# A two-block transformer kernel: first phase and first expert layer in one program block, and another order at the entry of the second attention

## The reference

```python
h = _layernorm(x) * (1 + ca) + sa
x = x + ga * _L0_attn_ref(h, W_qkv, W_out)           # linear attention, 16 heads of 8
h = _layernorm(x) * (1 + cb) + sb
x = x + gb * _L0_ffn_ref(h, ...)                     # the best of 8 experts per token, 128 -> 512 -> 128
h = _layernorm(x) * (1 + ca) + sa                    # modulation of block 1 from here
x = x + ga * _L1_attn_ref(h, Wqkv, Wproj, lambdas)   # differential attention, causal, 32 query and 8 key heads
# qkv = h @ Wqkv; softmax of q k^T / sqrt(8), pairs of heads subtracted with lambda, times v; two products with Wproj
h = _layernorm(x) * (1 + cb) + sb
x = x + gb * _L1_ffn_ref(h, ...)                     # the best two of 8 experts
```

## Time and profile before

| | us |
|---|---|
| median of 3 runs (643.12 to 646.38) | 644.96 |
| profiled execution | 643.2 |
| its span | 641.4 |
| PE busy | 513.7 |
| DVE busy | 422.1 |
| ACT busy | 335.7 |
| POOL busy | 320.8 |

### The profile page before, as it was taken

One profiled execution on the slowest core, in us unless ns is written; L12 is line 12 of the kernel. 1 busy time (PEld: TensorE's weight loads), 2 busy tenths in 40 slices (PEclk: granted clock), 3 DMA queues, 4 the chain that ended last, 5 costly groups with the idle time before them and its releaser, 6 DMA issues. The chain is left out here.

```text
span 641.4 us, 12683 instructions
## 1 busy us (share of the span) xinstructions
PE 513.7 (80%) x3814; PEld 349.8 (55%) x3814; DVE 422.1 (66%) x1650; ACT 335.7 (52%) x561; POOL 320.8 (50%) x481
## 2 busy tenths in 40 slices
PE   4977559970747999997999999999746199999970
PEld 2656449870323344543454444444445199999970
DVE  3775545446347979997899999993545745455436
ACT  5653325430752367775677777777434054444423
POOL 2541057772263356664468557754420267777630
PEclk9998569995687589998999999999955599999995
DMA  9300011123174445555544454332074011111205
GB/s 336 156 2 34 33 32 53 50 54 103 21 134 79 97 106 108 114 123 124 119 118 104 121 127 106 81 76 59 19 280 124 17 44 52 47 49 52 47 30 196
DMA packets 87899, 58.18 MB, mean 91 GB/s; under 512 B 72469, under 2 KB 73622, under 8 KB 85946
## 3 DMA queue, kind: packets, MB, share of 16 engines
q1 hardware_dynamic: 79258, 40.85, 25.5%
q0 software_dynamic: 3968, 8.13, 4.8%
q10 hardware_dynamic: 4608, 8.39, 3.7%
HBM read 37.72 MB, written 19.63 MB: 89 GB/s over the span
## 5 line engine op out<-in xcount | busy, mean ns | idle before, releaser
L1591 DVE CUSTOM_DVE_ANT_1 banks<-banks,a_mask 128x480 f32<-128x480 f32 (+14 forms) x480 | 190.0, 459 | 18.6 <-PE banks L1806 16.7
L1712 ACT ACTIVATE a_prob_<-banks 128x1024 f32<-128x1024 f32 x160 | 155.7, 1023 | 60.7 <-PE banks L1820 60.7
L1505 POOL TENSOR_SCALAR_AFFINE_SELECT a_prob_<-a_prob_ 128x512 f32<-128x512 f32 x128 | 81.0, 635 | 88.7 <-ACT a_prob_ L1712 88.6
L1806 PE MATMUL banks<-a_k_u_,a_q_u_ 72*128 72x512 bf16 (+15 forms) x512 | 109.2, 309 | 11.8 <-DMA a_k_u_<-scratch_k_parts 5.9
L1806 PEld LDWEIGHTS banks<-a_k_u_,a_q_u_ 72*128 72x128 bf16 x512 | 65.2, 149 | 81.8 <-DVE a_neg_max_ L1591 42.6
L1820 PE MATMUL banks<-a_q_u_,a_k_x_ 75*128 75x512 bf16 x320 | 102.2, 401 | 5.4 <-DMA a_q_u_<-scratch_m_rows 4.5
L1190 PE MATMUL banks<-f_hgt,f_w_now 128*112 128x128 f32 (+1 forms) x808 | 103.0, 279 | 0.4 <-DVE f_w_now L1013 0.3
L1190 PEld LDWEIGHTS banks<-f_hgt,f_w_now 128*112 128x112 f32 (+1 forms) x808 | 96.4, 185 | 1.3 <-DVE f_w_now L1013 0.8
L943 POOL DMA_INDIRECT f_hg<-scratch_h_rows,r_source x62 | 60.1, 970 | 71.6 <-DVE r_source L292 33.9
L1832 PE MATMUL banks<-a_prob_,a_v_g_ 128*32 128x512 f32 (+3 forms) x1024 | 86.0, 454 | 0.0
L949 POOL DMA_INDIRECT scratch_back_rows<-f_y,r_home x62 | 61.0, 984 | 35.3 <-DVE f_y L1039 26.5
(11 more groups left out here) (229 smaller groups left out, 633.6 us busy)
## 6 DMA issues: line engine op xcount, KB each, us to landing
a_q_u_<-scratch_q_parts SPq DMA_DIRECT2D x16, 576.0 KB
scratch_o_rows<-a_o_sb_ ACTq DMA_DIRECT2D x28, 256.0 KB, 2.6
w<-in_w SPq DMA_DIRECT2D x2, 2048.0 KB, 10.1
...
```

The costliest lines, as they stand in the source:

```text
L1505: nc.gpsimd.affine_select(out=block_p, in_=block_p, pattern=[[0, JH], [1, P]], compare_op=ALU.is_ge, fill=0.0, base=0, channel_multiplier= ...
L1591: last = nc.vector.tensor_tensor_reduce(out=found, in0=found, in1=mask[:, :, TG - 4 * (t + 1):], scale=-1.0, scalar=-MASKED, op0=ALU.add, ...
L1712: nc.scalar.activation(prob[g % 2][:, 2 * e:2 * e + 2].rearrange("p s j t c -> p (s j) t c"), PS[:, b0:b0 + 2, :].rearrange("p s (j c t) - ...
L1806: last = nc.tensor.matmul(PS[:, a % 3, off:off + width], queries[:, g % 2, :, t], k_u[r][:, :, g % 2 * TG:g % 2 * TG + 4 * (t + 1)], start ...
```

## The change

1. `phase_first` and the expert layer 0 become one program block: `experts_programs` returns the five engines' programs, and `phase_first` appends them to its own. The barrier between them goes; PE and ACT wait for the experts' numbers by a semaphore (`eid_ready`).
2. At the end of the first phase the lines of batch 2 are computed ahead of the residual of batch 3, `back` and `ranks` change places on PE, and two steps on ACT.
3. The loads of `back_rows`, the scaling and the addition move from the expert layer behind the barrier into the attention, batch by batch (`scaled_rows`, `added`), between the steps of the norm. Batch 0's norm is shared by ACT and DVE.
4. PE gets twenty products of constants (128x128 by 128x256, bfloat16, result unused) as soon as batch 0's rows have arrived, ahead of its first transposes.
5. Batch 0 goes through products and parts before batch 1; its lowest part is made on DVE (`lowest_first`); both of its first units are staged before batch 1's parts are written. The products of batches 2 and 3 each move behind one group of maxima.
6. On POOL the lowest parts of batch 3 and the weights scaled by the gate (`wproj_b`) move behind groups 1 and 2 of the loop.
7. In the loop SP issues `maxima_in(g + 1)` ahead of `stage`.
8. The query features of the first phase (`q_feat`) lie in the memory of `xn`, which is free by then.

The diff, without the re-indented body of the expert layer:

```diff
@@ -432,7 +432,7 @@
         qr = buf("qr", [P, B, T])
-        q_feat = buf("q_feat", [P, B, T])
+        q_feat = xn[:].rearrange("p (b i) d -> p b (i d)", i=NI)
@@ -461,6 +461,8 @@
         nd_of = PS[:, 4:6, :].rearrange("p a (c n) -> p (a c) n", c=2)
+        end_phase(sb)
+        sync, gpsimd, vector, scalar, tensor = experts_programs(nc, dram, sb, ps, 0, router, ctx)
@@ -615,8 +619,8 @@
             residual(2)
+            router.norm.lines(ve, 2)
             residual(3)
-            router.norm.lines(ve, 2)
@@ -701,10 +706,11 @@
             router.normalise(ac, 3)
+            router.rows_back(ac, 2)
             router.modulate(ac, 3)
-            router.rows_back(ac, 2)
...
             router.weights(ac)
+            scalar(ac)
@@ -840,16 +846,17 @@
             router.logits(pe, 2)
+            router.back(pe, 2)
...
             router.logits(pe, 3)
-            router.back(pe, 2)
+            router.ranks(pe, 1)
             router.back(pe, 3)
-            router.ranks(pe, 1)
...
-def phase_experts(nc, dram, sb, ps, layer, router):
+            tensor(pe)
...
+def experts_programs(nc, dram, sb, ps, layer, router, ctx):
@@ -1300,6 +1304,8 @@
         w_in, lam_in, wproj_ready = (semaphore(n) for n in ("w_in", "lam_in", "wproj_ready"))
+        back_in = [semaphore(f"back_in{b}_") for b in range(B)]
+        moved_ready, tail_ready, lo0_ready = (semaphore(n) for n in ("moved_ready", "tail_ready", "lo0_ready"))
@@ -1322,6 +1328,8 @@
         areas = ((P, slice(0, 2)), (D // 2, slice(2, 3)))
+        back = [at[b][:].rearrange("p (i d) -> p i d", i=NI) for b in range(B)]
+        moved = [o_b[b // 2][:, b % 2, :].rearrange("p (i d) -> p i d", i=NI) for b in range(B)]
@@ -1346,15 +1354,22 @@
             sp.dma_start(mask[:], dram["amask"]).then_inc(lam_in, 16)
+            for landed, count in sb["y_out"]:
+                sp.wait_ge(landed, count)
+            for b in range(B):
+                sp.dma_start(back[b], dram["back_rows"][b * T:(b + 1) * T, :].rearrange("(p i) d -> p i d", i=NI)
+                             ).then_inc(back_in[b], 16)
...
-                ready = (hi_ready, mid_ready, lo_ready)[n]
-                sp.wait_ge(ready, 2 * b + 1)
+                ready, of = (hi_ready, mid_ready, lo_ready)[n], b
+                if n == PARTS - 1:
+                    ready, of = (lo_ready, b - 1) if b else (lo0_ready, 0)
+                sp.wait_ge(ready, 2 * of + 1)
...
                                  part[b % 2][:, n, half, :].rearrange("f (u t) -> f u t", t=TG)).then_inc(parts_out[b], 16)
-                sp.wait_ge(ready, 2 * b + 2)
+                sp.wait_ge(ready, 2 * of + 2)
@@ -1428,20 +1443,23 @@
-            for b in range(2):
-                for n in range(PARTS):
-                    write_part(b, n)
-                stage(b)
+            for n in range(PARTS):
+                write_part(0, n)
+            stage(0)
+            stage(1)
             values(0)
+            for n in range(PARTS):
+                write_part(1, n)
...
             for g in range(GROUPS):
+                if g + 1 < GROUPS:
+                    maxima_in(g + 1)
...
                 if g + 1 < GROUPS:
-                    maxima_in(g + 1)
@@ -1525,15 +1543,11 @@
                 norm.deviations(gp, b)
-            gp.wait_ge(w_in, 2 * 16)
-            for b in range(B - 1):
-                lowest(b)
+            lowest(1)
...
             split_maxima(0)
-            lowest(B - 1)
-            for b in range(B):
-                nc.gpsimd.tensor_tensor(wproj_b[:, b, :], wproj[:], gates[:, b, 1, 0, :], ALU.mult).then_inc(wproj_ready, 1)
+            lowest(2)
@@ -1542,6 +1556,12 @@
                     causal(g, kb)
+                if g == 1:
+                    lowest(B - 1)
+                if g == 2:
+                    gp.wait_ge(w_in, 2 * 16)
+                    for b in range(B):
+                        nc.gpsimd.tensor_tensor(wproj_b[:, b, :], wproj[:], gates[:, b, 1, 0, :], ALU.mult).then_inc(wproj_ready, 1)
@@ -1556,12 +1576,44 @@
                 q = b % 2
-                if b >= 2:
-                    ve.wait_ge(lo_ready, 2 * (b - 1))
+                if b == 2:
+                    ve.wait_ge(lo0_ready, 2)
+                if b == 3:
+                    ve.wait_ge(lo_ready, 2)
...
+            def scaled_rows(b):
...
+                ve.wait_ge(back_in[b], 16)
+                for i in range(NI):
+                    t = b * NI + i
+                    ch.step(nc.vector.scalar_tensor_tensor(moved[b][:, i, :], back[b][:, i, :], sb["gate0"][:, 0, t:t + 1],
+                                                           gates[:, b, 0, 1, :], ALU.mult, ALU.mult))
...
+            def added(b):
...
+                ch.wait()
+                xb = x_sb[:, b * NI:(b + 1) * NI, :]
+                nc.vector.tensor_tensor(xb, xb, moved[b], ALU.add).then_inc(moved_ready, 1)
+                ve.wait_ge(moved_ready, b + 1)
+                norm.variances(ch, b)
...
+            def shared_rows():
...
+                for t in (2, 3):
+                    last = nc.vector.tensor_scalar(xn[:, t, :], x_sb[:, t, :], norm.mv[:, t, 0:1], norm.rstd[:, t:t + 1],
+                                                   ALU.subtract, ALU.mult)
+                last.then_inc(tail_ready, 1)
...
+            def lowest_first():
...
+                for n, (rows, at_) in enumerate(areas):
+                    ve.wait_ge(mid_ready, n + 1)
+                    nc.vector.tensor_tensor(part[0][0:rows, 2, at_], rest[0][0:rows, at_], part[0][0:rows, 1, at_],
+                                            ALU.subtract).then_inc(lo0_ready, 1)
@@ -1627,27 +1679,33 @@
-            norm.variances(ch, 0)
-            norm.variances(ch, 1)
+            scaled_rows(0)
+            added(0)
+            scaled_rows(1)
             norm.lines(ve, 0)
-            norm.variances(ch, 2)
+            shared_rows()
+            added(1)
+            scaled_rows(2)
             norm.lines(ve, 1)
-            norm.variances(ch, 3)
+            added(2)
             norm.lines(ve, 2)
-            norm.lines(ve, 3)
             remainders(0)
-            remainders(1)
-            remainders(2)
+            lowest_first()
+            scaled_rows(3)
+            added(3)
...
             nc.vector.memset(one_row[:], 1.0).then_inc(lam_sum, 1)
+            norm.lines(ve, 3)
+            remainders(1)
...
                 maximum(0, a)
+            remainders(2)
+            for a in range(NA):
+                maximum(1, a)
...
             coefficients()
-            for a in range(NA):
-                maximum(1, a)
@@ -1730,22 +1788,26 @@
-            norm.normalise(ac, 0)
+            ac.wait_ge(norm.line_ready, 1)
+            for t in (0, 1):
+                last = nc.scalar.activation(xn[:, t, :], x_sb[:, t, :], ACT.Identity, scale=norm.rstd[:, t:t + 1],
+                                            bias=norm.line[:, t:t + 1])
+            last.then_inc(norm.xn_ready, 1)
+            rows_t(0)
             norm.normalise(ac, 1)
-            rows_t(0)
+            highest(0)
+            middle(0)
...
             norm.normalise(ac, 2)
-            highest(0)
+            highest(1)
+            middle(1)
+            rows_t(2)
             norm.normalise(ac, 3)
-            middle(0)
-            highest(1)
-            rows_t(2)
-            middle(1)
-            highest(2)
             rows_t(3)
-            middle(2)
...
             nc.scalar.activation(lexp[:], lsum[:], ACT.Exp).then_inc(lam_exp, 1)
+            highest(2)
+            middle(2)
@@ -1834,24 +1898,29 @@
+            pe.wait_ge(back_in[0], 16)
+            for n in range(20):
+                nc.tensor.matmul(PS[:, 0, 0:2 * P], sb["ones"], sb["squares"][:].rearrange("p n c -> p (n c)"), start=True, stop=True)
...
             pe.wait_ge(w_in, 2 * 16)
-            for b in range(B - 1):
-                transposed(b + 1)
-                products(b)
+            products(0)
+            transposed(1)
+            products(1)
+            transposed(2)
+            transposed(3)
...
                 max_scores(0, a)
-            products(B - 1)
+            products(2)
+            for a in range(NA):
+                max_scores(1, a)
+            products(3)
...
             nc.tensor.matmul(PS[:, 7, 0:2], one_row[:], lexp[:], start=True, stop=True).then_inc(lam_mm, 1)
-            for a in range(NA):
-                max_scores(1, a)
...
             pe.wait_ge(fills, RING + 2 * VR)
-            pe.wait_ge(wproj_ready, B)
@@ -1887,6 +1956,8 @@
                     pe.wait_ge(upd_ready, b)
+                else:
+                    pe.wait_ge(wproj_ready, B)
...
```

589 lines of the change are left out of this document (295 added, 294 removed).

## The result

The changed kernel takes 628.46 us (median of 4, 627.51 to 629.26) where the kernel before took 645.67 beside it (median of 4, 643.12 to 648.41): a ratio of 0.973, interval 0.969 to 0.978. The forecast was 628.0. Its profiled execution took 628.5 us for a span of 626.7, 14.7 us less than the span of before.

What follows compares the result with a forecast made beforehand. Stages with different limits: POOL in the expert layer, PE in the attention loop. 3.1 + 0.8 + 5.7 - 0.4 + 7.2 = 16.4, plus 0.5: 16.9 us off 644.96 gives 628.1, said as 628, range 624.5 to 632.

Steps and rivals of the forecast that it cites:

- First phase: End of the first phase: batch 2's earlier line and the new PE order gain 3.1 us, bounds 2 and 5.
- first seam: Entry to the expert layer: without a barrier the first gather follows the row numbers directly, gaining 0.8 us.
- Loads behind the weights: Attention entry: semaphore clearing, barrier and SP's four weight loads make the expert rows 1.4 us later, bounds 0.8 and 3.
- T: Moment the expert rows' data is there at the attention's entry, forecast near 150.4 us in the old trace's time.
- First maxima: Attention entry: first row-maximum products at 179.1 us for 189.35, 10.2 us earlier, about 34 us after the last scatter's issue.
- What is given back: Attention entry: batch 3's products behind group 1 are uncovered, shrinking the gain from 10.2 to 5.7 us at first scores.
- The loop's loads: Attention loop: maxima issued ahead of the staging remove PE's stall; 7.2 us gained, bounds 3 and 7.8.
- Warm start of the loop: First groups of the attention loop: starting at full clock would gain about 0.5 us.
- A: Loop's stall stays or moves to the value rows; 7 us missing, 635 us; chance 0.15.
- B: Attention entry gives all back, batch 3's products costing 6 us more than reckoned; 634 us; chance 0.11.
- C: Loop starts at lasting full PE clock, DVE becomes the limit, about 4 us more saved; 624 us; chance 0.10.
- D: Slower than before: early loop groups stay at half clock, each costing 3.2 us; 650 us; chance 0.02.

Runs made afterwards that it cites:

- e5: Changed kernel with the line of batch 2 behind the residual of batch 3 again on DVE; 634.59 us, 0.984 of the kernel before.
- e4: Changed kernel with SP issuing the four loads of expert rows ahead of the four weight loads; 627.32 us, 0.973 of the kernel before.
- e3: Changed kernel without its twenty products of constants, on a slower chip; 655.41 us, 0.975 of the kernel before on that chip.
- e1: Changed kernel with the loop's staging ahead of the next group's maxima again, on a slower chip; 664.32 us, 0.987 of the kernel before there.
- e6: Changed kernel with the products of batches 2 and 3, and their remainders, one place earlier; 628.27 us, 0.974 of the kernel before.
- e2: Kernel before with one edit, the next group's maxima loaded ahead of the staging, on a slower chip; 661.35 us, 0.984 of the unedited kernel there.

## Why the prediction was right, and where its sum was not

The sum was 16.9 us, the traces give 14.7. That the time still came out within 0.5 us of the median is luck. The prediction started from a median 1.8 us above the profiled execution of before and carried this difference over; the changed kernel does not show it (profiled 628.5, median 628.46). With the 14.7 us of the traces the same working gives 630.3. The medians are 17.2 us apart, and where the slower executions of before lost the rest no trace shows. The mechanisms hold for the most part, and single terms missed both ways:

- **First phase, 3.1, and first seam, 0.8.** The total is right, 3.7 for 3.9, and so are the causes: the line (e5) and the barrier, 1.81 - 1.06 = 0.75 from the row numbers to the gather. The sizes within the phase cancelled. Batch 2's transposes came 3.63 us sooner, 0.46 of it since the batch ahead was sooner by that much (56.99 for 57.45). The new order on PE cost 7.33 - 6.40 = 0.93 up to the logits of batch 3, for 0.4, and gave back 0.27 behind them, for 0.4. So the logits at 70.10 (forecast 70.1) are luck in part.
- **Loads behind the weights, 1.4 us later.** T came 5.76 after the last scatter for 4.11, so 1.65 (forecast 5.5, measured 5.8). The weights' four issues, 1.5 us, are the cause: e4 takes it back. Ahead of them, the semaphore clearing and the barrier took 0.93 us together (141.39 to 142.32), where some 0.9 were reckoned.
- **First transposes, T + 5.8.** 5.76.
- **Twenty products, 0.2.** Right that they are hidden (4.45 us under a forecast bound of 5.0). In this trace they gave nothing, transposes and query products ran at half clock; in five others they may have given up to 0.9 us (e3, e4), within the bounds.
- **First maxima, 34.2 us after the last scatter.** 35.98: the term that was mis-sized. The last write before the staging was issued at 167.22 + 0.66 = 167.88, 26.5 us after the last scatter, where 169.9 - 144.91 = 25.0 was forecast. Of these 1.5 us T makes 0.3, query parts at T + 12.1 for 12.7 take 0.6 off, and SP's writes make 0.5. The rest, 1.3, is what was wrong in the working: it summed remainders, middle and lowest parts (4.2 us) as if one engine took over from the other at once, while the trace has 5.6 from the start of the highest part's cast to the end of the lowest, with DVE idle for 0.99 us ahead of the remainders (ACT's cast takes 1.01) and for 0.94 ahead of the lowest part (ACT's middle part). From the write to the maxima it took 9.5 us and not 8.7, and the 0.5 us that were to be lost to batch 3's transposes were not. In e1 and e3 another 1.2 us went with SP's issuing of the writes, so the 1.8 us in all are of the size of the scatter.
- **What is given back.** The step was right: from first maxima to first scores 24.1 us (forecast 23.8), and e6 shows the cause. So the entry is worth 3.6 at the first scores and not 5.7: 1.8 from the maxima, 0.3 from here. That it is worth as much at the end of the loop, as the sum takes for granted, is what e1 and e2 do not bear out.
- **The loop's loads, 7.2.** Mechanism right, shown from both sides by e1 and e2. The size of the one stall was wrong: 14.08 - 7.08 took the pace of the groups around it, but this group takes 8.11 even without a wait (as do two others, eight and sixteen groups later). 5.97, not 7.0; about 1.0 came from small waits of the same kind, where 0.4 was allowed, so 7.0 in all for 7.2.
- **Warm start of the loop, 0.5.** 0.9: the first scores ran at full clock (0.61 us for 1.01), granted 0.92 over their first 3.6 us.
- **POOL, 0.4.** Right: the value products of the third group wait 0.38 us for POOL, and the group that ends there takes 7.52 for 7.07.
- **Rivals.** A is refuted for this kernel (no DMA wait is left). B did not come: what was given back is 24.1 us for 23.8, and of the 2.1 us that the entry lacks 1.8 were lost ahead of the maxima. C did not come: the loop started at full clock and fell back, granted 0.55 over its first group with PE busy 13.19 of 13.30 us. Nor did D: the full clock came back at about 221.5 us, after some 17 us at half, for 20 before.
